# Attention with its fill products in four 32-column quarters, its weight gathers spread and its tail on buffers of its own

## The chip, the cores and the metric

The kernel runs on all 8 cores of one Trainium2 chip, four to a die (cores 0 to 3 and 4 to 7). Each core works alone on its share of the tokens; nothing is exchanged. The metric is the device time of the slowest core in microseconds, as the median of several runs.

## The reference

A sandwich of two residual layers on x of 4 x 4096 x 1024, float32:

```python
x = x + _layernorm(attn(_layernorm(x)))     # 16 heads of 64; Wq, Wk, Wv, Wp, each 1024 x 1024
x = x + _layernorm(ffn(_layernorm(x)))      # one of 8 matrices W[idx], 1024 x 1024, and b[idx]
```

In attn a key takes part if it is not later than the query and its position modulo 4 is not 3; the scores are scaled by 1/8. In ffn, idx is the argmax of log_softmax(logits) plus Gumbel noise made from u, so the matrix is known only at run time.

## The kernel before, in words

Two cores share a batch entry. Each takes every second query (2048) and all 3072 keys that are kept. Work is in bfloat16 with float32 sums.

The **lead** (`lead_units`) transposes the first ten 128-token tiles on TensorE ("T" units), and makes keys of groups 0 and 1 ("K"), values ("V"), the queries of stage 0 ("Q"), norms of both ("N") and from these a bound ("C", the `prodm` product) that goes into each exp as its bias `negc`. Then come four **stages**, one for each 512 queries. Stage t has 8 head pairs of 3t + 2 **pairs of steps**, so 16, 40, 64 and 88 pairs, 208 in all. A step is 128 keys (or two parts of the diagonal) by 512 queries for two heads. A pair goes so:

- `qk(m)`, L725 and L727: scores of both steps, two products of 64 rows by 128 columns side by side. The second buffer is free once the exp of two steps before is done (`s_exp`).
- fills: a part of a `unit`. A unit is a full 128 x 128 product over 8 chunks of the contraction: K (384 wide, L666), Q (L675), V (L682), O, the projection (L701), F, the ffn (L710), each into one of two `pj` banks. Stages 0 to 2 are filled with the next stage's Q, K, V, norm and C units, stage 3 with O and F of query tiles 0 to 11.
- `pv(m-1)`, L762: values. Each of four 128 x 32 products has its own quarter of the columns, with `tile_position=(0, j)`.
- `rowsum(m-1)`, L780: sums of the exps, also in four quarters.

ScalarE does the exps (L1208, 128 x 1024) and part of the evictions; VectorE the other evictions and layer norms; GpSimd masks the diagonal steps (L1320) and issues the weight loads with a cast; SP issues token loads, DMA transposes and stores.

The order of every engine is written by a planner, `make_order`. `spread` lays the fills evenly over 0.94 of a stage's pairs (0.98 in stage 3); `clock` estimates when each pair begins, and every other operation gets a due time, by which the engine queues are sorted. `UNIT_N` numbers the units in TensorE's order; the first `LEAD` of them belong to the lead.

The ffn weights `wfb` lie where `wkb` was. GpSimd gathers them by eight indirect DMAs of 128 rows each (L1388), one behind another, once the last key unit ("K", 7, 7) is done.

The **tail** is the four last query tiles, 12 to 15. `tail_o` makes their projection, `tail_z` and `tail_x` the statistics and the first residual, `tail_ln` the third layer norm, a DMA transpose turns it (SP, "turn"), `tail_f` makes the ffn product (L826 and L828), `tail_fs` and `tail_froot` its statistics, `tail_last` (VectorE, L1085) multiplies and adds, `tail_out` (ScalarE, L1256) subtracts the mean, and the result is stored. The tiles share two staging and two transposed buffers (`ln3t[s % 2]`, `ln3T[s % 2]`), so that the third transpose waits for the first tile's product.

Of the kernel before, what the change touches and what calls it, by code (L numbers as in the profile page):

```python
# [94 lines left out]
def lead_units():  # L95
# [7 lines left out]
    out += v0[:2] + t[6:7] + nk[2:3] + v0[2:4] + t[7:8] + nk[3:] + v0[4:] + t[8:9] + v1[:2] + t[9:]  # L103
    out += q + v1[2:3] + nq[:1] + v1[3:4] + nq[1:] + v1[4:5] + [("C", 0)] + v1[5:]
# [71 lines left out]
def make_order():  # L176
# [133 lines left out]
    z_at, x_at, f_at, last_at = [0.0, 1.4, 5.2, 9.0], [2.8, 6.6, 10.4, 12.8], [15.2, 18.6, 22.0, 26.0], [17.4, 21.0, 24.5, 28.3]  # L310
    for j, s in enumerate(TAIL):
# [7 lines left out]
        dve.append((at + last_at[j], "taillast", s))  # L319
        act.append((at + last_at[j] + 0.6, "tailout", s))  # L320
# [5 lines left out]
    pool.append((end["K", 7, 7] + 0.5, "wf", 0))  # L326
# [54 lines left out]
def build_nc():  # L381
# [109 lines left out]
    ln3t = [ln3, over("ln3t", [128, C], BF16, "wvb", 8192)]  # L491
# [19 lines left out]
    def sem(name):  # L511
        return nc.alloc_semaphore(name=name)
# [83 lines left out]
    s_tfin = sem("s_tfin")  # L596
    s_tdone = sem("s_tdone")
# [24 lines left out]
    def tensor_engine():  # L622
# [31 lines left out]

        def unit(part):
# [5 lines left out]
            if u[0] == "K":  # L661
# [3 lines left out]
                for c in range(c0, c1):  # L665
                    mm = PE.matmul(ps[:, 0:384], wkb[:, c, 128 * e:128 * e + 128], fm[g % 2][:, c, :],  # L666
                                   start=(c == 0), stop=(c == 7))
            elif u[0] == "Q":
# [3 lines left out]
                for c in range(c0, c1):  # L672
                    if t == 0 and e == 0 and c % 4 == 0:
                        PE.wait_ge(s_w["wq", c // 4], 16)
                    mm = PE.matmul(ps[:], wqb[:, c, 128 * e:128 * e + 128], fmQ[:, c, :],  # L675
                                   start=(c == 0), stop=(c == 7))
            elif u[0] == "V":
                _, g, sc, eh = u
                for c in range(c0, c1):
                    if (g, sc, eh) == (0, 0, 0) and c % 4 == 0:  # L680
                        PE.wait_ge(s_w["wv", c // 4], 16)
                    mm = PE.matmul(ps[:], fm[g % 2][:, c, 128 * sc:128 * sc + 128],  # L682
                                   wvb[:, c, 512 * eh:512 * eh + 512], start=(c == 0), stop=(c == 7))
# [9 lines left out]
            elif u[0] == "O":  # L693
# [4 lines left out]
                for c in range(c0, c1):  # L698
                    if s == 0 and eh == 0 and c % 4 == 0:
                        PE.wait_ge(s_w["wp", c // 4], 16)  # L700
                    mm = PE.matmul(ps[:], QY[:, t, c, 128 * j:128 * j + 128],  # L701
                                   wpb[:, c, 512 * eh:512 * eh + 512], start=(c == 0), stop=(c == 7))
            else:
# [3 lines left out]
                for c in range(c0, c1):  # L707
                    if s == 0 and eh == 0:
                        PE.wait_ge(s_wf[c], 16)
                    mm = PE.matmul(ps[:], ln3T[s % 2][:, c, :],  # L710
                                   wfb[:, c, 512 * eh:512 * eh + 512], start=(c == 0), stop=(c == 7))
# [110 lines left out]
        def tail_f(s):  # L822
            PE.wait_ge(s_turn[s % 2], 16 * (s // 2 + 1))
# [723 lines left out]
```

## Time and profile before

| | |
|---|---|
| Three runs, median (lowest, highest) | 762.2 us (761.1 to 763.1) |
| Profiled execution | 765.7 us |
| its span, slowest core (core 1) | 764.6 us |
| its fastest core | 749.4 us |
| TensorE matmuls busy | 669.8 us, 5716 instructions |
| ScalarE busy | 528.8 us |
| VectorE busy | 422.9 us |
| GpSimd busy | 137.5 us |
| instructions in all | 17094 |

The profile is of one execution, on its slowest core unless another is named. In the rows PE is TensorE, PEld its weight loads, DVE VectorE, ACT ScalarE, POOL GpSimd and SP the queue that issues most DMAs. A matmul's start is a time of the profiler, its end is modelled, so costs of matmuls are best read from start to start. "<-" behind a wait names what ended it.

### The profile page before, as it was taken

Reading aid. Unit: us, or ns where it says so; the run is one execution under the profiler, and the core shown is the slowest. Engines: PE = TensorE matmul, PEld = TensorE weight load, DVE = VectorE, ACT = ScalarE, POOL = GpSimd, SP = SyncE. Lnnn points to the kernel's source line nnn. Section 1 sums busy time; section 2 is a strip of 40 time slices with the busy share of each in tenths; the row PEclk is TensorE's granted clock in tenths of the full one; section 3 lists DMA queues with packets and bytes.
Section 4 is the critical chain, followed back from the end, with each engine's and each line's share of the span. In section 5 each row is a group of like instructions: output and inputs, shape, how many; then the busy total and the mean of one; then the engine's idle time right before and its main releaser. Section 6 shows DMA issues by size and latency. Waiting matters only on the chain.

```text
span 764.6 us, 17094 instructions; the slowest of 8 cores (749.4 to 764.6 us)
## 1 busy us (share of the span) xinstructions
PE 669.8 (88%) x5716; PEld 254.0 (33%) x5716; DVE 422.9 (55%) x758; ACT 528.8 (69%) x710; POOL 137.5 (18%) x232
## 2 busy tenths in 40 slices
PE   1788979898999999999999859889999999999855
PEld 1444434343333343333323313222333333332322
DVE  3337667857463634533433213267766766986496
ACT  3342356454898786988787648888888888888246
POOL 1010022223112221112121411110120110750100
PEclk9989999999999999999999979999999999999988
DMA  8889488961653160307000160502222223133314
GB/s 164 177 197 182 99 152 188 181 154 34 150 110 86 28 143 16 72 16 111 27 6 16 40 100 23 174 15 61 79 84 86 71 84 111 30 114 96 119 34 138
DMA packets 78211, 72.00 MB, mean 94 GB/s; under 512 B 58544, under 2 KB 58800, under 8 KB 78128
## 3 DMA queue, kind: packets, MB, share of 16 engines
q1 hardware_dynamic: 72060, 59.50, 30.7%
q0 software_dynamic: 5696, 11.14, 9.4%
q8 instruction: 49, 0.80, 0.4%
q10 hardware_dynamic: 372, 0.27, 0.1%
q14 instruction: 34, 0.28, 0.1%
HBM read 60.68 MB, written 8.52 MB: 90 GB/s over the span
## 4 chain that ended last, share of the span: by engine, by line
PE 59%; ACT 12%; issue 11%; DVE 8%; DMA 6%; another core or an unknown queue 2%; ACTq 1%; SPq 1%; DVEq 0%; POOL 0%; POOLq 0%
PE sps L725 11%; PE yz L762 10%; ACT Pr L1208 9%; PE pj L666 9%; PE pj L682 8%; PE pj L675 5%; PE pj L710 4%; PE yz L780 4%; PE pj L701 4%; DMA zr<-zev 2%; DMA xin<-xkv 1%; DMA fmQ<-tok 1%; PE yz L682 1%; PE yz L675 1%
## 5 line engine op out<-in xcount | busy, mean ns | idle before, releaser
L1208 ACT ACTIVATE Pr<-sps,negc 128x1024 bf16<-128x1024 f32 (+1 forms) x416 | 429.6, 1079 | 115.3 <-PE sps L727 100.0
L1320 POOL TENSOR_TENSOR Pr<-Pr,mk_sb 128x172 bf16<-128x172 bf16 x192 | 100.4, 542 | 497.7 <-ACT Pr L1208 497.6
L725 PE MATMUL sps<-QY,Ksb 64*128 64x512 bf16 (+2 forms) x480 | 137.2, 346 | 23.6 <-ACT Pr L1208 19.1
L727 PE MATMUL sps<-QY,Ksb 64*128 64x512 bf16 (+2 forms) x480 | 138.9, 349 | 0.0
L762 PE MATMUL yz<-Pr,Vsb 128*32 128x512 bf16 (+5 forms) x1920 | 126.5, 349 | 4.7 <-DVE yev L960 2.4
L780 PE MATMUL yz<-Pr,cbf 128*32 128x512 bf16 (+2 forms) x960 | 82.0, 345 | 4.7 <-issue 4.7
L725 PEld LDWEIGHTS sps<-QY,Ksb 64*128 64x128 bf16 x480 | 35.5, 93 | 130.1 <-issue 127.4
L882 DVE TENSOR_TENSOR Vsb<-pj,bvb 128x512 bf16<-128x512 f32 x41 | 28.2, 688 | 68.9 <-PE pj L682 50.4
L762 PEld LDWEIGHTS yz<-Pr,Vsb 128*32 128x32 bf16 x1920 | 31.3, 95 | 86.5 <-issue 84.9
L675 PE MATMUL pj<-fmQ,wqb 128*128 128x512 bf16 x224 | 54.7, 385 | 3.3 <-DMA fmQ<-tok 1.9
L701 PE MATMUL pj<-wpb,QY 128*128 128x512 bf16 x192 | 50.4, 381 | 0.2 <-issue 0.2
L682 PE MATMUL pj<-wvb,fmA 128*128 128x512 bf16 x168 | 41.7, 380 | 5.3 <-DVE Vsb L882 5.3
L666 PE MATMUL pj<-fmB,wkb 128*128 128x384 bf16 x232 | 44.3, 336 | 1.4 <-ACT fmB L1154 1.3
L960 DVE COPY yev<-yz 128x512 f32<-128x512 f32 x32 | 22.1, 690 | 37.6 <-PE yz L780 37.6
L682 PE MATMUL pj<-wvb,fmB 128*128 128x512 bf16 x160 | 40.6, 392 | 0.7 <-DVE Vsb L882 0.7
L666 PE MATMUL pj<-fmA,wkb 128*128 128x384 bf16 x192 | 36.5, 327 | 4.4 <-ACT Ksb L1187 2.1
L1187 ACT ACTIVATE Ksb<-pj,bkc 128x384 bf16<-128x384 f32 x39 | 22.3, 577 | 21.4 <-PE pj L650 11.5
L872 DVE TENSOR_SCALAR tok<-xin,lnst 128x1024 bf16<-128x1024 f32 x33 | 27.9, 846 | 14.4 <-ACT lnst L1150 13.1
L727 PEld LDWEIGHTS sps<-QY,Ksb 64*128 64x128 bf16 x480 | 35.6, 93 | 0.0
L780 PEld LDWEIGHTS yz<-Pr,cbf 128*32 128x32 bf16 x960 | 25.5, 97 | 25.8 <-issue 6.7
L675 PEld LDWEIGHTS pj<-fmQ,wqb 128*128 128x128 bf16 x224 | 19.7, 99 | 32.7 <-issue 14.0
L973 DVE TENSOR_TENSOR QY<-yev,zb 128x512 bf16<-128x512 f32 x32 | 22.8, 712 | 13.6 <-DMA zb<-zscr 13.3
(187 smaller groups left out, 767.4 us busy)
## 6 DMA issues: line engine op xcount, KB each, us to landing
xin<-xkv SPq DMA_DIRECT2D x21, 512.0 KB, 4.8
xr<-xq SPq DMA_DIRECT2D x16, 512.0 KB, 3.4
zb<-zscr SPq DMA_DIRECT2D x62, 128.0 KB, 3.0
xin<-xq SPq DMA_DIRECT2D x12, 512.0 KB, 3.9
out<-xr SPq DMA_DIRECT2D x12, 512.0 KB, 2.9
wkb<-wk POOLq DMA_DIRECT2D x4, 512.0 KB, 17.4
wvb<-wv POOLq DMA_DIRECT2D x2, 1024.0 KB, 14.8
wqb<-wq POOLq DMA_DIRECT2D x2, 1024.0 KB, 14.0
```

Source lines behind the costliest of these rows:

```text
L666: mm = PE.matmul(ps[:, 0:384], wkb[:, c, 128 * e:128 * e + 128], fm[g % 2][:, c, :], start=(c == 0), stop=(c == 7))
L675: mm = PE.matmul(ps[:], wqb[:, c, 128 * e:128 * e + 128], fmQ[:, c, :], start=(c == 0), stop=(c == 7))
L682: mm = PE.matmul(ps[:], fm[g % 2][:, c, 128 * sc:128 * sc + 128], wvb[:, c, 512 * eh:512 * eh + 512], start=(c == 0), stop=(c == 7))
L701: mm = PE.matmul(ps[:], QY[:, t, c, 128 * j:128 * j + 128], wpb[:, c, 512 * eh:512 * eh + 512], start=(c == 0), stop=(c == 7))
L710: mm = PE.matmul(ps[:], ln3T[s % 2][:, c, :], wfb[:, c, 512 * eh:512 * eh + 512], start=(c == 0), stop=(c == 7))
L725: PE.matmul(sps[s % 2][:, 0, off:off + w], Ksb[0:64, g, hp, kc:kc + 128], QY[0:64, t, hp, n0:n0 + w], start=True, stop=True, tile_position ...
L727: mm = PE.matmul(sps[s % 2][:, 1, off:off + w], Ksb[64:128, g, hp, kc:kc + 128], QY[64:128, t, hp, n0:n0 + w], start=True, stop=True, tile ...
L762: PE.matmul(yps[j:j + 32, n0:n0 + w], Vsb[:, c, 64 * h + 32 * half:64 * h + 32 * half + 32], Pr[:, s % 4, hd, off:off + w], start=first, s ...
L780: mm = PE.matmul(zps[j:j + 32, n0:n0 + w], cbf[:, 288:320], Pr[:, (2 * m + a) % 4, hd, off:off + w], start=first and not (a == 1 and k < 8 ...
L882: V.tensor_tensor(out=Vsb[:, 3 * g + sc, 512 * eh:512 * eh + 512], in0=ps[:], in1=bvb[:, 512 * eh:512 * eh + 512], op=ALU.add).then_inc(s_ ...
L1208: A.activation(out=Pr[:, s % 4, :, 0:wide], in_=sps[s % 2][:, :, 0:wide], func=AF.Exp, bias=negc[:, k:k + 1], scale=0.125).then_inc(s_exp, 1)
L1320: op = G.tensor_tensor(out=view, in0=view, in1=mk[:, j:j + 1, :].broadcast_to([128, 2, BAND]), op=ALU.mult)
```

## The change

1. A new function `product` takes the place of the plain matmul in K, Q, V, O and F units behind the lead: four matmuls of 32 columns, each with its tile position.
2. The eight gathers become eight entries of GpSimd's queue, due 5 us apart by the planner, each waiting for the exps that are due before it.
3. In the lead, the values of group 1 go behind the queries, and the first query norm comes in among them.
4. In the tail each tile has staging and transposed buffers of its own, with semaphores of their own, so that `tail_ln` and the transposes wait for no earlier tile. Two small operations per tile leave VectorE for ScalarE. For tiles 12 to 14 the last step is split in another way: ScalarE scales and shifts the product out of PSUM (`tail_scale`), GpSimd adds it to the residual (`tail_sum`); tile 15 keeps the old way. The due times of the last steps follow.

```diff
@@ lead_units
-    out += v0[:2] + t[6:7] + nk[2:3] + v0[2:4] + t[7:8] + nk[3:] + v0[4:] + t[8:9] + v1[:2] + t[9:]
-    out += q + v1[2:3] + nq[:1] + v1[3:4] + nq[1:] + v1[4:5] + [("C", 0)] + v1[5:]
+    out += v0[:2] + t[6:7] + nk[2:3] + v0[2:4] + t[7:8] + nk[3:] + v0[4:5] + t[8:9] + v0[5:] + t[9:]
+    out += q[:7] + nq[:1] + q[7:] + v1[:2] + nq[1:] + v1[2:4] + [("C", 0)] + v1[4:]
@@ make_order
-    ..., f_at, last_at = ..., [15.2, 18.6, 22.0, 26.0], [17.4, 21.0, 24.5, 28.3]
+    ..., f_at, last_at = ..., [15.2, 16.6, 18.0, 22.0], [17.2, 18.6, 20.2, 24.0]
...
+        if s < 15:
+            act.append((at + last_at[j], "tailscale", s))
+            pool.append((at + last_at[j] + 0.6, "tailsum", s))
...
-    pool.append((end["K", 7, 7] + 0.5, "wf", 0))
+    for c in range(8):
+        at = end["K", 7, 7] + 0.5 + 5.0 * c
+        done = sum(begin[m] + 0.4 + 1.1 * a < at for m in range(NP) for a in range(2))
+        pool.append((at, "wf", (c, done)))
@@ tensor_engine
+        def product(u, ps, w, left, right, c):
+            if UNIT_N[u] <= LEAD:
+                return PE.matmul(ps[:, 0:w], left, right, start=(c == 0), stop=(c == 7))
+            for j in range(0, 128, 32):
+                mm = PE.matmul(ps[j:j + 32, 0:w], left[:, j:j + 32], right, start=(c == 0), stop=(c == 7),
+                               tile_position=(0, j))
+            return mm
...
-                    mm = PE.matmul(ps[:, 0:384], wkb[:, c, 128 * e:128 * e + 128], fm[g % 2][:, c, :],
-                                   start=(c == 0), stop=(c == 7))
+                    mm = product(u, ps, 384, wkb[:, c, 128 * e:128 * e + 128], fm[g % 2][:, c, :], c)
...
@@ tail_f
-            PE.wait_ge(s_turn[s % 2], 16 * (s // 2 + 1))
+            PE.wait_ge(s_tturn[s - 12], 16)
@@ tail_x
-            V.tensor_tensor(out=st[:, 48:49], in0=st[:, 12:13], in1=st[:, 15:16], op=ALU.mult).then_inc(s_tx, 1)
...
-            V.tensor_scalar(out=st[:, 49:50], in0=st[:, 28:29], scalar1=-1.0, scalar2=None,
-                            op0=ALU.mult).then_inc(s_txst, 1)
@@ tail_ln
-            if s == 13:
-                A.wait_ge(s_x1, 23)
-            else:
-                A.wait_ge(s_turn[(s - 2) % 2 if s > 12 else 1], 16 * (6 if s == 12 else (s - 2) // 2 + 1))
...
-            A.activation(out=ln3t[s % 2][:], in_=xr[s % 4][:], func=AF.Identity, bias=st[:, 50:51],
+            A.activation(out=st[:, 50:51], in_=st[:, 49:50], func=AF.Identity, scale=-1.0).then_inc(s_txroot, 1)
+            A.wait_ge(s_txroot, 3 * j + 3)
+            A.activation(out=ln3t[j][:], in_=xr[s % 4][:], func=AF.Identity, bias=st[:, 50:51],
@@ scalar_engine
+        def tail_scale(s):
+            j = s - 12
+            A.wait_ge(s_tfroot, 3 * j + 3)
+            for eh in range(2):
+                A.activation(out=tfo[j][:, eh, :], in_=tail_ps[j][:, eh, :], func=AF.Identity,
+                             bias=tst[:, j, 52:53], scale=tst[:, j, 47:48]).then_inc(s_tscale, 1)
@@ pool_engine
+        def tail_sum(s):
+            j, x = s - 12, xr[s % 4]
+            for eh in range(2):
+                half = x[:, 512 * eh:512 * eh + 512]
+                G.wait_ge(s_tscale, 2 * j + eh + 1)
+                G.tensor_tensor(out=half, in0=half, in1=tfo[j][:, eh, :], op=ALU.add).then_inc(s_tsum, 1)
...
+                c, done = key
+                if c == 0:
+                    G.wait_ge(s_sel, 8)
+                    G.wait_ge(s_unit, UNIT_N["K", 7, 7])
+                G.wait_ge(s_exp, done)
+                G.indirect_dma_start(out=wfb[:, c, :], out_offset=None, in_=wf_d,
+                                     in_offset=IndirectOffsetOnAxis(gcol[:, c:c + 1], 0)
+                                     ).then_inc(s_wf[c], 16)
@@ sync_engine
-                if key >= 14:
-                    S.wait_ge(s_ft, 2 * (key - 13))
-                elif key >= 2:
+                if 2 <= key < 12:
                     S.wait_ge(s_unit, UNIT_N["F", key - 2, 1])
```

Q, V, O and F units get the same treatment as K, with a width of 512.

## Rows read from the trace of the kernel before

**Rows 1.** The page: busy time of TensorE's matmuls; the chain's shares by engine.
```profile
PE 669.8 (88%) x5716; PEld 254.0 (33%) x5716; DVE 422.9 (55%) x758; ACT 528.8 (69%) x710; POOL 137.5 (18%) x232
...
PE 59%; ACT 12%; issue 11%; DVE 8%; DMA 6%; another core or an unknown queue 2%; ACTq 1%; SPq 1%; DVEq 0%; POOL 0%; POOLq 0%
```

**Rows 2.** The view of cores: span and granted clock.
```profile
core 1: 764.6 us, clock 0.976
...
core 4: 753.7 us, clock 0.976
```

**Rows 3.** The view by windows, 430 to 460 us, core 1 then core 4.
```profile
430.00:460.00 30.00, 19.78 (x146) 6.14 (x144) 5.03 (x9) 13.86 (x14) 9.83 (x13) 0.83 0.48 80
...
430.00:460.00 30.00, 28.64 (x282) 9.57 (x280) 10.43 (x22) 24.75 (x25) 12.39 (x19) 1.00 0.53 81
```

**Rows 4.** The timeline, GpSimd, 430 to 470 us: the first and last of 8 gathers.
```profile
433.68 1.03 POOL L1388 DMA_INDIRECT wfb<-wf,gcol  x1 [0.85 <-PE pj L666]
...
442.29 0.94 POOL L1388 DMA_INDIRECT wfb<-wf,gcol  x1 [0.27 <-issue]
```

**Rows 5.** The waits, 400 to 500 us: total us, times, longest.
```profile
ACT Pr L1208 <- remote: 11.8, 2, 9.0
```

**Rows 6.** The timeline, TensorE, 701 to 704 us, second scores to next scores.
```profile
701.51 0.37 PE L725 MATMUL sps<-QY,Ksb 64*128 64x512 bf16 x1
...
701.84 1.25 PE L710 MATMUL pj<-wfb,ln3Tb 128*128 128x512 bf16 x5
703.02 0.62 PE L762 MATMUL yz<-Pr,Vsb 128*32 128x512 bf16 x8
703.46 0.39 PE L780 MATMUL yz<-Pr,cbf 128*32 128x512 bf16 x4
703.78 0.39 PE L725 MATMUL sps<-QY,Ksb 64*128 64x512 bf16 x1
```

**Rows 7.** The timeline of the tail: last ffn products, last tile's statistics.
```profile
752.36 1.89 PE L828 MATMUL yz<-wfb,ln3Tb 128*128 128x512 bf16 x8
...
754.30 1.89 PE L828 MATMUL yz<-wfb,ln3Tb 128*128 128x512 bf16 x8
...
757.57 1.28 DVE L1076 BATCH_NORM_STATS2 tst<-yz 128x6 f32<-128x512 f32 x2
```

**Rows 8.** The timeline, TensorE, 425 to 427 us, key chunks and the values behind.
```profile
425.17 1.15 PE L666 MATMUL pj<-fmB,wkb 128*128 128x384 bf16 x6
426.24 0.61 PE L762 MATMUL yz<-Pr,Vsb 128*32 128x512 bf16 x8
```

**Rows 9.** The timeline, TensorE, 712 to 714 us, quarters just after a wait.
```profile
713.04 0.37 PE L762 MATMUL yz<-Pr,Vsb 128*32 128x256 bf16 x8 [0.53 <-POOL Pr L1320]
713.23 0.37 PE L780 MATMUL yz<-Pr,cbf 128*32 128x342 bf16 x8
713.63 0.38 PE L787 MATMUL pj<-brow,bsel 128*128 128x512 bf16 x1
```

**Rows 10.** The page's groups: the weight loads of the values, mean ns of one.
```profile
L762 PEld LDWEIGHTS yz<-Pr,Vsb 128*32 128x32 bf16 x1920 | 31.3, 95 | 86.5 <-issue 84.9
```

**Rows 11.** The waits of TensorE, 310 to 485 us, then 485 to 711 us.
```profile
PE sps L725 <- ACT Pr L1208: 7.7, 20, 1.1
...
PE sps L725 <- ACT Pr L1208: 9.6, 29, 1.0
```

**Rows 12.** The timeline, TensorE, 90 to 98 us: the end of the lead.
```profile
90.68 1.90 PE L682 MATMUL yz<-wvb,fmB 128*128 128x512 bf16 x8
93.09 0.40 PE L688 MATMUL yz<-ksq,cbf 128*32 128x512 bf16 x4 [0.51 <-DVE ksq L904]
93.42 1.90 PE L682 MATMUL pj<-wvb,fmB 128*128 128x512 bf16 x8
97.60 0.17 PE L692 MATMUL pj<-prodm,cbf 128*128 128x8 bf16 x1 [2.27 <-DVE prodm L922]
```

**Rows 13.** The groups by form, GpSimd: a float32 addition of 1024 elements.
```profile
L1339 POOL TENSOR_TENSOR brest<-bfb,brow 128x1024 f32<-128x1024 f32 x1 | 2.1, 2127 | 0.1
```

## What the change will do

> **What bounds the kernel now.** I read the page first, then the cores, then one stretch at a time. The page: TensorE's matmuls cover 88% of the span, and the chain that ended last runs through TensorE for 59% of it, with ScalarE second at 12% [rows 1]. So most of the span belongs to the order in which TensorE takes its work, and a nanosecond saved in each step of it is worth looking for.
>
> The cores come next, because the metric is the slowest. Core 1 sets the time with 764.6; the slowest core of the other die, core 4, has 753.7 [rows 2]. All eight run one program on equal amounts of work, so most of these 10.9 us are lost on one die only. They go between 430 and 460 us: core 1's TensorE is busy 19.78 us of 30 at clock 0.83, core 4's 28.64 at 1.00, with the same DMA share of about 0.5 [rows 3]. In this stretch GpSimd issues the eight gathers of the ffn weights one behind another, one every 1.2 us, from 433.68 to 442.29 [rows 4]; the first mask behind them waits for ScalarE, so GpSimd itself isn't late. ScalarE stood for 11.8 us in two waits that the profile puts down to nothing on the core [rows 5]. I read this as traffic: eight transfers queued at once, and whatever the engines fetch meanwhile stands behind them.
>
> Within a steady pair of steps near 701 us the start times give TensorE's cost of each piece [rows 6]: second scores at 701.51, fills at 701.84, values at 703.02, sums at 703.46, next scores at 703.78. Five fill chunks take 1.18 us to the values' start. A chunk is 0.216 by the tail (eight and one in 1.94 us, 752.36 to 754.30) [rows 7], so 5 x 0.216 = 1.08 and 0.10 is left over. The same comes from the key units: six 384-wide chunks take 1.07 us to the values [rows 8]; at 0.16 each (384/512 of 0.216) that is 0.97, and 0.10 is left. The scores stand 0.33 ahead of the fills and the sums 0.32 ahead of the next scores, where a group of the values takes 0.22. So each change between kinds of array use costs about 0.1 us, and a pair has three: scores (64 rows) to fills (128 x 128), fills to values (128 x 32), sums to scores.
>
> **The change, part by part.** *Fills as quarters.* Each of the 156 units behind the lead has 8 chunks, 1248 in all; a chunk becomes four matmuls of 32 columns, so 3744 matmuls and as many weight loads are added. The fill-to-values change disappears, since both are then 128 x 32. The planner spreads fills over 0.94, 0.94, 0.94 and 0.98 of 16, 40, 64 and 88 pairs: 15 + 38 + 60 + 87 = 200. At 0.095 that is 19.0 us. The 18 norm units behind the lead are quarters already and stand among the fills, with a change on either side; those at the edge of a pair share theirs, so I count some 22 further, 2.1 us. The three bound products stay full width and now have a change in front as well, +0.3 us. Gross on TensorE: 20.8 us.
>
> What does a quartered chunk cost? The trace of before has no such fill, but values and sums have its form. Eight value matmuls (two groups) take 0.44 us, 703.02 to 703.46 [rows 6]: 0.22 a group, beside 0.216 for a full chunk. I take 0 extra; the upper bound is the remainder, 0.01 a chunk, about 13 us over 1248. Below nothing I see no reason. Can TensorE be given eight instructions in 0.216, or in 0.16 for keys? After a wait of 0.53 us, when nothing was queued ahead, 16 matmuls and their loads pass between 713.04 and 713.63 [rows 9]: 32 instructions in 0.59 us, 18 ns each, against 27 and 20 needed. It is enough, for keys only just. A weight load has a mean of 95 ns [rows 10] and must lie beside matmuls: in the value groups four of them fit into 0.22 us, so they do.
>
> *How much of 20.8 us arrives.* TensorE isn't alone in the loop. Two exps of a pair take about 2.12 us, the next but one first score product follows from them, and where the second one of a pair waits for the exp, a fill shorter by 0.1 us is paid back by half at most, as the loop then spans two pairs with one fill in it. Such waits are recorded 20 times from 310 to 485 us and 29 times from 485 to 711 us, 7.7 and 9.6 us [rows 11], and pairs that are just short of them now will begin to wait. So: stage 0 (16 pairs, fed by transposes and by VectorE) half of 2.0, 1.0 us; stage 1 nearly all of its 4.4, less the bound product, 3.8; stage 2 two thirds of 5.9, 3.9; stage 3 two thirds of 8.3, 5.5; the other bound products -0.2. Sum 14.0 us. Bounds: 7 (a third) to 21.
>
> *Gathers spread.* Each of the eight now waits for a count of exps, 5 us behind the one before. Queued behind each on GpSimd are masks, at most one of which is held by an issue of 1.2 us per gather, and values wait a step and a half later; I take 1 us in all for that and for what stays of the traffic. The last gather starts about 35 us behind the first, near 470 us, and the first ffn product is far behind. If the stall goes, core 1 falls to the slowest of the undisturbed die: 764.6 - 753.7 = 10.9, less 1.0, is 9.9 us. Bounds: 3 (it is only thinned) to 11.
>
> *Values behind queries in the lead.* Now the second norm product waits 0.51 us at 93.09 and the bound product 2.27 us at 97.60 [rows 12], since only two value units lie between the last query unit and it. After the change two stand ahead of the second norm product and two more ahead of the bound product, 3.45 us each (two units of 8 x 0.216). The gap at the bound product spans 95.15 to 97.60, the one at the norm product 92.41 to 93.09, so 2.45 + 0.68 = 3.1 us go. The transposes for the next queries are issued once the last query unit is done, and that moves forward by as much (two value units, 3.45, less the one norm product now inside the queries, 0.33), so stage 0 is not left waiting for them: 3.1 us. Bounds 0 to 3.4. The token for the ninth transpose is ready long before, but ScalarE's copy in front of the queries stays bare.
>
> *The tail.* It is VectorE's now: the last tile's products end at 756.2 (754.30 and 1.89), yet its statistics begin only at 757.57 [rows 7]. Three of the four final multiplications leave VectorE for ScalarE and GpSimd; eight small operations go too; with own buffers no transpose waits for products. TensorE's chain of four ffn tiles, 3.9 us each, then sets the end. The last tile's first-half statistics could start by 755.7, as their second half needs 756.3 and one takes about 0.65. 757.57 - 755.7 = 1.8 us. The GpSimd additions, 512 wide, I put at 1.1 us each (half of 2.13 for 1024) [rows 13]; two of tile 14 behind ScalarE end near 758, before the end of tile 15. ScalarE's two additional small operations ahead of each transpose are covered but for some 0.3. Bounds 0.5 to 3.
>
> **Sum.** 764.6 - 14.0 - 9.9 - 3.1 - 1.8 = 735.8 of span; outside it this execution had 1.1 us (765.7), so 736.9. The median shown, 762.2, is 3.5 below this execution; the stall is what differs among cores, so I expect runs with less of it to have less to gain, and leave the forecast at 737.
>
> **Rivals.** (1) The stall stays or moves. TensorE's stream of instructions grows by 7488 on 17094, so more is fetched, and a fetch behind a gather still stands. For: 11.8 us of waits without a source on the core [rows 5]. Against: die 1 has the same gathers and no loss [rows 3]. Price: 5 to 9 us of the 9.9, so 742 to 746. (2) ScalarE's loop takes all in stages 2 and 3: 9.4 us less, 746. For: the waits [rows 11]; against: they are in fewer than half of the pairs. (3) The quarters cost 0.01 more each, 13 us: 750. (4) **Slower**: the four weight loads of a chunk aren't hidden in an unbroken row of fills. Gains of 28.8 us over 1248 chunks are used up at 23 ns each; one bare load of 95 ns a chunk would cost 119 us, and the time would be 856. For: the trace shows at most 24 quartered matmuls in a row between waits. Against: 0.22 a group where values stand [rows 6] and the burst [rows 9]. (5) That the quarters don't remove the change, as the tiles' positions differ by 32 columns within it: values and sums alternate over four positions at 0.22 without any, so I give it nothing apart from (2).
>
> A rule speaks for (4). The Trainium skill's page TensorE: Matmul & The Clock Gate, section The mechanism (Part 3), says that a weight load overlaps running matmuls only where it goes to other row groups; all quarters here span all rows. By that, and by its figure of columns over 1.2 GHz, four loads of 32 columns would add an estimated 107 ns a chunk, some 133 us. The Trainium skill's page TensorEngine Tiling (Array Packing), section Restrictions, adds that column tiling goes without the fast weight load. This case's values contradict the first: 0.22 us a group in the same form [rows 6].
>
> **Chances.** Forecast with its own bounds (729 to 742): 0.60. Rival 1: 0.15. Rival 2: 0.09. Rival 3: 0.08. Rival 4: 0.04, of it nearly all slower. More gained than I allow, under 729: 0.04. Range 729 to 751: it takes in rivals 1 to 3. A measurement of this kernel can tell about 0.3%, 2.3 us, from no change. Faster 0.95, same 0.01, slower 0.04.
>
> **What would show it.** In the profile after: fill matmuls of form 128*32, starts of groups 0.216 apart (0.16 for keys), last fill to values 0.22 instead of 0.31; more waits of the scores on exps in the last two stages; 430 to 470 us with TensorE at clock 1.00 on every core and the dies within a few us; bound product in the lead without its 2.27 us wait; tail with TensorE running to its last ffn product and VectorE's last statistics right behind. Wrong if groups stand at 0.24 or more, if the dies stay 10 us apart, or if ScalarE's idle time does not shrink from 485 to 711 us.

## The result, and the profile after

The changed kernel takes 743.5 us (three runs, 743.47 to 744.73) against 762.2 us (761.14 to 763.13): a ratio of 0.976, 95% interval 0.974 to 0.979. The gain is 18.7 us where 25 were forecast; the time lies 6.5 us above the 737.0 forecast and inside the range of 729 to 751. In some executions of any of these kernels one die shows a lower granted clock and the time is longer (807.6 and 825.3 us for e1_quarters, 809.1 for e3_lead); no comparison below uses them.

The page of the profiled execution after, with its busy times, the instruction fetches, the chain's shares by engine, and the group of the first score product:

```profile
span 741.9 us, 24587 instructions; the slowest of 8 cores (733.8 to 741.9 us)
PE 653.2 (88%) x9460; PEld 284.6 (38%) x9460; DVE 418.6 (56%) x744; ACT 530.2 (71%) x718; POOL 145.0 (20%) x238
...
q8 instruction: 79, 1.29, 0.7%
...
PE 54%; ACT 15%; issue 15%; DMA 8%; DVE 5%; SPq 1%; POOL 1%; ACTq 1%; DVEq 0%; POOLq 0%
...
L744 PE MATMUL sps<-QY,Ksb 64*128 64x512 bf16 (+2 forms) x480 | 138.4, 346 | 25.0 <-ACT Pr L1223 22.9
```

Against [rows 1], matmuls are busy 16.6 us less, with 3744 more of them (the two pages are of different cores, 1 and 6). TensorE's share of the chain falls from 59 to 54% and ScalarE's rises from 12 to 15%. The last row matters most below: 22.9 us of idle before the first score product are ended by an exp. Line numbers have moved: L673 is now the one line of all quartered fills, L744 and L746 are the scores, L781 values, L799 sums, L1223 exps, L1354 masks, L1427 gathers.

The view of cores, after, beside [rows 2]:

```profile
core 1: 733.8 us, clock 0.984
...
core 4: 741.3 us, clock 0.979
...
core 6: 741.9 us, clock 0.975
...
die 0 (median of its cores): 736.2 us, clock 0.983
die 1 (median of its cores): 740.5 us, clock 0.977
```

Core 1, the slowest before, has won 30.8 us and is now the fastest. Core 6, the fastest before at 749.4 us, has won 7.5 and sets the time. To see where, I split each core's span at the starts of its exps in the timeline of ScalarE: the 1st exp, and those of pairs 17, 57 and 121, which begin stages 1 to 3 (exps 33, 113 and 241), and the last (416th). Each column is one execution:

| us | before, core 1 | after, core 1 | before, core 6 | after, core 6 | median of 8, before to after |
|---|---|---|---|---|---|
| first exp | 100.0 | 94.3 | 99.6 | 97.7 | 99.5 to 96.0 |
| stage 0 | 90.0 | 90.5 | 91.0 | 94.4 | 91.3 to 92.6 |
| stage 1 | 120.0 | 117.2 | 118.8 | 116.1 | 120.0 to 117.2 |
| stage 2 | 174.2 | 157.9 | 159.3 | 157.8 | 164.7 to 157.9 |
| stage 3 | 226.6 | 222.2 | 226.2 | 222.4 | 226.3 to 222.1 |
| tail, from the start of the last exp | 53.8 | 51.7 | 54.4 | 53.4 | 54.2 to 52.0 |

Stages 1 to 3 are now nearly the same on all cores (stage 2 takes 157.8 to 158.6 us, where die 0 had 168.8 to 174.2). What separates the cores most is what comes before stage 1: its first exp starts between 184.1 and 192.4 us. The tail adds up to 2 us (51.7 to 53.9).

**A pair of the last stage.** The timeline of TensorE, core 6, five chunks of fill as in [rows 6]:

```profile
679.80 1.26 PE L673 MATMUL pj<-wfb,ln3Tb 128*32 128x512 bf16 x20
680.89 0.61 PE L781 MATMUL yz<-Pr,Vsb 128*32 128x512 bf16 x8
681.32 0.39 PE L799 MATMUL yz<-Pr,cbf 128*32 128x512 bf16 x4
681.64 0.39 PE L744 MATMUL sps<-QY,Ksb 64*128 64x512 bf16 x1
681.65 0.39 PE L746 MATMUL sps<-QY,Ksb 64*128 64x512 bf16 x1
682.07 0.37 PE L744 MATMUL sps<-QY,Ksb 64*128 64x512 bf16 x1
```

Twenty quarters take 1.09 us to the values (679.80 to 680.89), where five full chunks took 1.18. Over all pairs of core 0 the starts of groups of four stand 0.216 us apart in the median (0.163 for products 384 wide), and from the last group to the values it is 0.216 where it was 0.309. But the second pair of scores starts 0.43 us behind the first, where 0.226 is the shortest: it stood for the exp that ends at 681.93 in ScalarE's timeline.

**The gathers.** The timeline of GpSimd, core 6, beside [rows 4]; then 430 to 460 us by windows, core 1 and core 4, beside [rows 3]; then ScalarE's waits on core 1, 400 to 500 us, beside [rows 5]:

```profile
429.15 1.04 POOL L1427 DMA_INDIRECT wfb<-wf,gcol  x1 [1.46 <-ACT Pr L1223]
...
443.93 0.94 POOL L1427 DMA_INDIRECT wfb<-wf,gcol  x1 [3.93 <-ACT Pr L1223]
444.89 2.75 POOL L1354 TENSOR_TENSOR Pr<-Pr,mk_sb 128x172 bf16<-128x172 bf16 x6
...
463.01 0.94 POOL L1427 DMA_INDIRECT wfb<-wf,gcol  x1 [3.06 <-ACT Pr L1223]
```
```profile
430.00:460.00 30.00, 25.27 (x361) 9.02 (x357) 9.27 (x20) 24.76 (x28) 11.58 (x18) 1.00 0.58 125
...
430.00:460.00 30.00, 27.42 (x411) 10.15 (x399) 11.12 (x24) 25.23 (x27) 9.48 (x13) 1.00 0.44 67
```
```profile
ACT Pr L1223 <- PE sps L746: 14.4, 23, 1.3
```

The clock is 1.00 on both dies, ScalarE runs 24.76 us of 30 instead of 13.86, and the two waits that the profile calls "remote" (11.8 us) are gone.

**The lead.** The timeline of TensorE, core 1 and then core 6, beside [rows 12]:

```profile
90.27 0.17 PE L712 MATMUL pj<-prodm,cbf 128*128 128x8 bf16 x1
90.30 1.89 PE L671 MATMUL pj<-wvb,fmB 128*128 128x512 bf16 x8
...
97.09 4.07 PE L673 MATMUL pj<-fmQ,wqb 128*32 128x512 bf16 x72 [2.68 <-DMA fmQ<-tok]
```
```profile
55.54 5.30 PE L671 MATMUL yz<-wvb,fmA 128*128 128x512 bf16 x16 [2.73 <-ACT Ksb L1202]
...
93.25 0.17 PE L712 MATMUL pj<-prodm,cbf 128*128 128x8 bf16 x1
```

The bound product waits no more on either core. Core 6 is 3.0 us behind core 1 there, from one place, before which it was 1.0 us ahead: at 55.54 it had stood 2.73 us for an eviction, and then took 5.30 us for sixteen products which take 3.63 on core 1; its granted clock was 0.50 from 57 to 60 us.

**The tail.** The timeline of TensorE and VectorE on core 1, then TensorE on core 5, beside [rows 7]; and GpSimd's first addition on core 1:

```profile
710.83 3.04 PE L847 MATMUL pj<-wfb,ln3Tt 128*128 128x512 bf16 x8
...
725.57 1.89 PE L847 MATMUL yz<-wfb,ln3Tt 128*128 128x512 bf16 x8
...
727.57 0.70 DVE L1091 BATCH_NORM_STATS2 tst<-yz 128x6 f32<-128x512 f32 x1 [1.24 <-PE yz L847]
```
```profile
711.60 3.62 PE L847 MATMUL pj<-wfb,ln3Tt 128*128 128x512 bf16 x8
...
727.50 1.89 PE L847 MATMUL yz<-wfb,ln3Tt 128*128 128x512 bf16 x8
```
```profile
721.28 2.49 POOL L1346 TENSOR_TENSOR xr<-xr,yev 128x512 f32<-128x512 f32 x2 [37.14 <-ACT yev L1272]
```

On core 1 TensorE runs from tile to tile without a gap, and VectorE's last statistics now wait for it. From the first tile's first eight products (710.83) to the last tile's last eight (725.57) it is 14.7 us; on core 5 it is 15.9, since its granted clock is 0.50 until 716 and the first tile runs longer. Behind the last product 6.3 to 6.8 us are left on all cores, where it was 7.2 to 8.8 before: most of the tail's gain lies there.

### The profile page after: what moved, and what is told of

It reads as the page before. It is cut to its first block, busy times and chain, and to the rows that moved or that the text cites. A ratio compares the mean times of both kernels' runs of the same rounds, so it can differ in the third digit from the quotient of the medians.

```text
span 741.3 us, 24579 instructions; the slowest of 8 cores (733.8 to 741.9 us)
## 1 busy us (share of the span) xinstructions
PE 649.0 (88%) x9452; PEld 283.8 (38%) x9460; DVE 418.1 (56%) x744; ACT 530.2 (72%) x718; POOL 144.0 (19%) x238
## 4 chain that ended last, share of the span: by engine, by line
PE 50%; ACT 15%; issue 15%; DMA 11%; DVE 6%; SPq 1%; ACTq 1%; POOL 1%; DVEq 0%; POOLq 0%
PE pj L673 23%; ACT Pr L1223 12%; PE sps L744 10%; PE yz L781 7%; PE yz L799 4%; DMA wkb<-wk 3%; DMA wvb<-wv 2%; PE yz L671 2%; DMA fmQ<-tok 1%; PE pj L671 1%; PE sps L847 1%; DVE Vsb L901 1%; DMA zr<-zev 1%; DMA xq<-xkv 1%; DMA xq<-xq 1%
## 5 line engine op out<-in xcount | busy, mean ns | idle before, releaser
L1223 ACT ACTIVATE Pr<-sps,negc 128x1024 bf16<-128x1024 f32 (+1 forms) x416 | 428.8, 1078 | 92.7 <-PE sps L746 90.1
L1354 POOL TENSOR_TENSOR Pr<-Pr,mk_sb 128x172 bf16<-128x172 bf16 x192 | 98.9, 536 | 464.8 <-ACT Pr L1223 464.7
L744 PE MATMUL sps<-QY,Ksb 64*128 64x512 bf16 (+2 forms) x480 | 138.7, 346 | 25.2 <-ACT Pr L1223 23.2
L746 PE MATMUL sps<-QY,Ksb 64*128 64x512 bf16 (+2 forms) x480 | 140.4, 350 | 0.0
L781 PE MATMUL yz<-Pr,Vsb 128*32 128x512 bf16 (+5 forms) x1920 | 125.0, 345 | 5.8 <-POOL Pr L1354 3.2
L744 PEld LDWEIGHTS sps<-QY,Ksb 64*128 64x128 bf16 x480 | 35.8, 93 | 133.5 <-issue 131.2
L799 PE MATMUL yz<-Pr,cbf 128*32 128x512 bf16 (+2 forms) x960 | 82.0, 345 | 0.0
L781 PEld LDWEIGHTS yz<-Pr,Vsb 128*32 128x32 bf16 x1920 | 49.4, 97 | 49.3 <-issue 12.5
L673 PE MATMUL pj<-wpb,QY 128*32 128x512 bf16 x768 | 50.7, 381 | 0.1
L673 PE MATMUL pj<-fmQ,wqb 128*32 128x512 bf16 x768 | 48.0, 388 | 2.2 <-DMA fmQ<-tok 2.2
L673 PE MATMUL pj<-wvb,fmA 128*32 128x512 bf16 x576 | 38.2, 394 | 5.0 <-DVE Vsb L901 5.0
L673 PE MATMUL pj<-fmA,wkb 128*32 128x384 bf16 x768 | 36.7, 327 | 3.8 <-ACT Ksb L1202 2.5
L673 PE MATMUL pj<-wvb,fmB 128*32 128x512 bf16 x576 | 35.5, 381 | 0.8 <-DVE Vsb L901 0.8
L673 PE MATMUL pj<-fmB,wkb 128*32 128x384 bf16 x768 | 36.0, 327 | 0.1
L746 PEld LDWEIGHTS sps<-QY,Ksb 64*128 64x128 bf16 x480 | 36.1, 93 | 0.0
L992 DVE TENSOR_TENSOR QY<-yev,zb 128x512 bf16<-128x512 f32 x32 | 23.9, 748 | 16.6 <-DMA zb<-zscr 16.4
L799 PEld LDWEIGHTS yz<-Pr,cbf 128*32 128x32 bf16 x960 | 25.8, 97 | 19.5 <-issue 0.9
L673 PEld LDWEIGHTS pj<-fmQ,wqb 128*32 128x32 bf16 x768 | 18.5, 98 | 26.6 <-issue 13.0
```

Source lines behind the costliest of these rows:

```text
L673: mm = PE.matmul(ps[j:j + 32, 0:w], left[:, j:j + 32], right, start=(c == 0), stop=(c == 7), tile_position=(0, j))
L744: PE.matmul(sps[s % 2][:, 0, off:off + w], Ksb[0:64, g, hp, kc:kc + 128], QY[0:64, t, hp, n0:n0 + w], start=True, stop=True, tile_position ...
L746: mm = PE.matmul(sps[s % 2][:, 1, off:off + w], Ksb[64:128, g, hp, kc:kc + 128], QY[64:128, t, hp, n0:n0 + w], start=True, stop=True, tile ...
L781: PE.matmul(yps[j:j + 32, n0:n0 + w], Vsb[:, c, 64 * h + 32 * half:64 * h + 32 * half + 32], Pr[:, s % 4, hd, off:off + w], start=first, s ...
L799: mm = PE.matmul(zps[j:j + 32, n0:n0 + w], cbf[:, 288:320], Pr[:, (2 * m + a) % 4, hd, off:off + w], start=first and not (a == 1 and k < 8 ...
L992: V.tensor_tensor(out=QY[:, t, hp, :], in0=yev[:, k % 2, :], in1=zb[:, k % 2, :], op=ALU.mult).then_inc(s_ynorm, 1)
```

## The experiments

Numbers of stages below are medians over the eight cores. "Before" was timed again on the chip of each group of runs.

**1. The parts alone.** Four kernels, each the kernel before with one part of the change. Only the lines that matter are shown.

```diff
e1_quarters: K, Q, V, O and F units by
+            for j in range(0, 128, 32):
+                mm = PE.matmul(ps[j:j + 32, 0:w], left[:, j:j + 32], right, start=(c == 0), stop=(c == 7),
+                               tile_position=(0, j))
```

> The kernel before with the quartered fills alone. Theory A (the quarters' 20.8 us on TensorE arrive for about a third, since the exps' loop takes the rest): 7 to 9 us less than before, about 754, with the stall of the gathers still there and the dies still some 10 us apart. Rival B (they arrive for two thirds, as predicted, and another part of the change gave less): 13 to 15 us less, about 748. Rival C (a stream of 44% more instructions suffers more from the gathers' traffic): under 5 us less, with the stall longer than before on die 0 or on both dies.

Two runs gave 756.3 and 761.0 us, where before gave 763.2 to 769.0 on that chip. That is too few for a ratio, so I read the profiled run by stage: stage 0 92.7 (no gain), stage 1 117.0 (120.0 in the profile of before, 118.8 in that of the next kernel), stage 3 222.2 (4 less); stage 2 on die 1 156.7 (2.7 less) and on die 0 166.3, still with the stall. This is nearest to theory A. The stall isn't longer (7.6 to 7.8 us a core, 6.6 to 11.8 before), against rival C. No group of quarters costs more than the full chunk did. That ends rival 3 (0.01 us more each) and rival 4 (bare weight loads, 856 us).

```diff
e2_gathers:
-    pool.append((end["K", 7, 7] + 0.5, "wf", 0))
+    for c in range(8):
+        at = end["K", 7, 7] + 0.5 + 5.0 * c
+        done = sum(begin[m] + 0.4 + 1.1 * a < at for m in range(NP) for a in range(2))
+        pool.append((at, "wf", (c, done)))
```

> The kernel before with the gathers spread alone. Theory A (the stall is the traffic of eight queued gathers, on die 0 only): core spans of die 0 fall to those of die 1, die 1 stays; time 8 to 10 us less, about 753. Rival B (the stall is something of die 0 that only happens to fall there): the dies stay some 10 us apart, time within 2 us of before.

758.1 us, ratio 0.989 (0.985 to 0.993): 8.4 us (5.4 to 11.2). Stage 2 takes 160.5 to 161.2 us on all cores. It was 168.8 to 174.2 on die 0 and 159.3 to 160.7 on die 1, so the stall is gone, and the spreading itself costs about 1.3 us (medians of die 1: 159.4 to 160.6).

```diff
e3_lead:
-    out += q + v1[2:3] + nq[:1] + v1[3:4] + nq[1:] + v1[4:5] + [("C", 0)] + v1[5:]
+    out += q[:7] + nq[:1] + q[7:] + v1[:2] + nq[1:] + v1[2:4] + [("C", 0)] + v1[4:]
```

> The kernel before with values behind queries alone. Theory A: the first exp comes about 3 us earlier, 97 instead of 100 us, and the time falls by 2 to 3 us. Rival B (stage 0 hangs on its transposes and tokens, and gives the 3 us back before stage 1): the first exp earlier, stage 1 at the same time as before, time within 1 us.

762.6 us, ratio 0.996 (0.994 to 0.999): 2.8 us (0.9 to 4.7), near the 3.1 forecast. The timeline of TensorE, core 1:

```profile
90.50 0.17 PE L692 MATMUL pj<-prodm,cbf 128*128 128x8 bf16 x1
...
97.78 3.57 PE L675 MATMUL pj<-fmQ,wqb 128*128 128x512 bf16 x8 [3.02 <-DMA fmQ<-tok]
```

The bound product is 7 us earlier than in [rows 12] and doesn't wait, but the first fill of stage 0 then stands 3.02 us for the transposes of the next queries, where it stood 1.9 before. In the median over the cores the first exp comes 3.1 us earlier and stage 1 begins 1.7 us earlier (190.7 to 189.0): stage 0 gives part of the gain back, as rival B said, but not all.

```diff
e4_tail: buffers of their own, scaling on ScalarE, addition on GpSimd, nothing else
+    tfo = [yev, zev, zb]
+    ln3t = [over(f"ln3t{i}", [128, C], BF16, "QY", 8192 + 2048 * i) for i in range(4)]
+    ln3Tt = [over(f"ln3Tt{i}", [128, 8, 128], BF16, "QY", 16384 + 2048 * i) for i in range(4)]
```

> The kernel before with the new tail alone. Theory A (TensorE's chain of four ffn tiles becomes the bound): from the last exp to the end 52 us instead of 54, time 1.8 us less. Rival B (it depends on when TensorE's clock comes back after 9 us of idle time): 0 to 2.5 us by core, since with own buffers nothing else is left in front of it, and the slowest core may have none of it.

763.5 us, ratio 0.9965 (0.994 to 0.999): 2.7 us (1.0 to 4.4). Its tail is 52.2 us, from 51.7 to 53.6, against 54.2 before.

**2. The quarters, with everything else in place.** The changed kernel with full-width fills.

```diff
e5_after_full:
-            for j in range(0, 128, 32):
-                mm = PE.matmul(ps[j:j + 32, 0:w], left[:, j:j + 32], right, ..., tile_position=(0, j))
-            return mm
+            return PE.matmul(ps[:, 0:w], left, right, start=(c == 0), stop=(c == 7))
```

> The changed kernel with fills at full width again, everything else of the change kept. Theory A (the quarters arrive for under half of TensorE's 20.8 us): 8 to 10 us slower than the changed kernel, about 752, of it 4 in stage 3, 2 to 3 in stage 2, 2 in stage 1, none in stage 0. Rival B (14 us arrive): about 757.

752.7 us (751.9 to 754.2), ratio 0.985 (0.983 to 0.986). By medians the quarters are worth 9.2 us (752.7 less 743.5); by the two ratios, each against its own runs of before, 6.5. The last three stages, which are free of the lead's spread, give 1.5, 2.9 and 4.1, in sum 8.6 us before rounding. Over all profiled executions with whole exps, those with quarters against those with full fills, stage 1 differs by 1.6 us in the median and 2.3 in the mean, and stage 3 by 4.1 and 4.2. The prediction had 14.0. The row of the page for the first score product:

```profile
L739 PE MATMUL sps<-QY,Ksb 64*128 64x512 bf16 (+2 forms) x480 | 136.9, 346 | 18.9 <-ACT Pr L1218 16.5
```

It stands 16.5 us for exps with full fills and 22.9 with quarters: 6.4 us of the saving have turned into this wait. These are the slowest cores of two executions; averaged over the eight cores, such waits are 2.0, 5.2 and 9.6 us in stages 1 to 3 with full fills and 2.6, 7.6 and 12.8 with quarters. To check the books of one stage I summed, on core 0, the shortest spacing of each kind of neighbouring groups over stage 3: 203.3 us with full fills and 194.3 with quarters, 8.9 less before rounding. (These two sums depend somewhat on how kinds are told apart.) Between the two pairs of scores the time beyond the shortest spacing grows from 18.6 us (55 times) to 23.0 (58 times). 8.9 less 4.4 is 4.5, and the stage is 4.1 shorter.

**3. Is it the exps?** If that wait takes the saving back, shorter exps should let it through. In both kernels each exp covers half its columns (the other half of the tile holds ones).

```diff
e6_short, e7_full_short:
+            wide = wide // 2
             A.activation(out=Pr[:, s % 4, :, 0:wide], in_=sps[s % 2][:, :, 0:wide], func=AF.Exp,
```

> The changed kernel with each exp over the first half of its columns only (the other half of the weights stays at 1, so the output isn't the reference's). Theory A (the scores' wait for the exps takes what the quarters save): with exps of half the length nothing waits for them; stage 3 takes about 196 us instead of 222, which is what its TensorE groups add up to, and stage 2 about 138. Rival B (VectorE or the evictions hold the loop): stage 3 stays over 210 us.

> The same short exps, with fills at full width. Theory A: stage 3 takes 8 to 9.5 us longer than with quarters and short exps (87 changes of 0.093 and the values' groups), against 4.1 with whole exps; stage 2 some 6 us longer. Rival B (the loop isn't the reason; the saving of a pair is itself only 0.05): stage 3 about 4 us longer as with whole exps.

The times are 712.0 us with quarters and 723.2 with full fills, one run each: 11.2 us. Neither expectation came true as it stood. With quarters stages 2 and 3 take 146.2 and 203.7 us, not the 138 and 196 of theory A, and stage 3 does not stay over 210 as rival B has it; full fills make them 4.3 and 5.1 us longer, where theory A had 6 and 8 to 9.5 and rival B 4 in stage 3. By stage the quarters give 3.3, 4.3 and 5.1, in sum 12.8 us before rounding, where they gave 8.6 with whole exps. The 5.1 is loose: stage 3 differs by 4.6 us among the cores of the one execution and by 6.4 among those of the other. The page's rows, quarters first:

```profile
L744 PE MATMUL sps<-QY,Ksb 64*128 64x512 bf16 (+2 forms) x480 | 126.2, 350 | 2.5 <-ACT Pr L1225 2.1
```
```profile
L739 PE MATMUL sps<-QY,Ksb 64*128 64x512 bf16 (+2 forms) x480 | 124.5, 348 | 1.6 <-ACT Pr L1220 1.1
```

The wait is nearly gone in both, and 4.2 us more arrive. So ScalarE's loop does take part of the saving; it explains about 4 us of the 11 that are missing against the sum of shortest spacings (an estimate of 20.0 us for stages 1 to 3 from core 0: 4.5, 6.6 and 8.9). With half exps 12.8 of those arrive. The last 7 are not in one wait. In stage 3 of core 0 idle beyond the shortest spacings is 7.1 us with full fills and 11.5 with quarters, spread over scores to scores (1.5 to 3.1), fill to fill (1.1 to 2.8) and smaller ones. I have no cause for these that a run has shown.

**4. How far must the gathers stand apart?** The changed kernel with the gathers in one row, in two rows of four, and 2.5 us apart.

```diff
e11_together:
-        at = end["K", 7, 7] + 0.5 + 5.0 * c
...
+    pool.append((end["K", 7, 7] + 0.5, "wf", 0))
e10_fours:
+        at = end["K", 7, 7] + 0.5 + 20.0 * (c // 4)
e9_spacing:
+        at = end["K", 7, 7] + 0.5 + 2.5 * c
```

> The changed kernel with the eight gathers in one row again, the rest of the change kept. Theory A (the stall is that row's, whatever else changed): stage 2 at 165 to 170 us on die 0 and 156.5 on die 1, the slowest core some 8 us above the changed kernel, about 750. Rival B (die 0 lost time for another reason): as the changed kernel.

> The changed kernel with the gathers in two rows of four, 20 us apart. If the stall starts only with a long queue: stage 2 within 1 us of 157.9 on both dies. If it goes with the bytes that are queued: two stalls of together 4 to 9 us on die 0.

> The changed kernel with the gathers due 2.5 us apart instead of 5. At 5 us stage 2 takes 157.9 us on every core, 1.4 more than 156.5, which die 1 had with quarters and the gathers in one row. Theory A (the stall needs more than two or three gathers queued, and the 1.4 us are the masks behind gathers and longer traffic): stage 2 at 156.5 to 157.5 on both dies, time 0 to 1 us less than the changed kernel. Rival B (the stall comes from any gather's traffic that overlaps the next): the stall is back on one die, stage 2 over 160 there.

| gathers | time, us | stage 2, die 0 | stage 2, die 1 |
|---|---|---|---|
| eight in a row | 753.1 (one run) | 165.1 to 170.2 | 156.4 to 157.6 |
| two rows of four | 746.3 (one run) | 164.3 to 166.6 | 156.4 to 159.2 |
| 2.5 us apart | 746.3 (742.4 to 749.3) | 157.2 to 158.6 | 157.2 to 159.3 |
| 5 us apart (the change, other chip) | 743.5 | 157.8 to 158.6 | 157.8 to 157.9 |

ScalarE's waits on core 1 from 400 to 500 us, eight in a row and then two rows of four; and eight in a row by windows, core 1:

```profile
ACT Pr L1220 <- remote: 11.3, 3, 7.0
```
```profile
ACT Pr L1223 <- remote: 7.9, 2, 4.1
```
```profile
430.00:460.00 30.00, 22.04 (x242) 7.10 (x242) 6.11 (x11) 14.42 (x14) 9.28 (x14) 0.77 0.50 80
```

Four in a row stop ScalarE on all four cores of die 0 twice, 7.3 to 7.9 us in sum. Eight in a row stop it on all 20 cores of die 0 in the five kernels that have them (before, e1_quarters, e3_lead, e4_tail, e11_together), 4.7 to 11.8 us in sum. At 2.5 or 5 us apart no core of eight kernels has such a wait. So what is queued together matters, not that the same transfers run. On the 20 cores of die 1 with eight in a row ScalarE has no such wait; one of them (core 4 of e3_lead) lost about 6 us at the same place, where TensorE stood 4.5 us for VectorE and VectorE 8.8 us for the small DMA `zr<-zev`. Why mostly one die suffers, though both issue the same gathers, no run here tells.

"Remote" is only the profile's word for a wait whose end it can't place. In the kernel an exp waits for `s_qk` and `s_pv`, and TensorE alone raises both. So in those waits ScalarE waited for TensorE's counts, and the prediction's reading, nothing on the core, is wrong. The timeline of TensorE in the kernel before, core 1, and its DMA queues from 441.8 to 465.7 us:

```profile
441.11 0.37 PE L725 MATMUL sps<-QY,Ksb 64*128 64x512 bf16 x1 [2.27 <-issue]
...
446.63 0.38 PE L780 MATMUL yz<-Pr,cbf 128*32 128x512 bf16 x1 [2.07 <-issue]
449.65 0.63 PE L780 MATMUL yz<-Pr,cbf 128*32 128x512 bf16 x3 [2.65 <-issue]
```
```profile
q0 software_dynamic: 747, 1.34, 35.6%
q1 hardware_dynamic: 365, 0.27, 4.2%
```

TensorE stands three times, 7.0 us in all, for nothing that the profile shows ("issue"), and ScalarE's wait ends at 449.97. On core 3 no such gap is drawn: TensorE's matmuls end by 443.6 and the exp starts at 448.99. That the stopped engine waits for its instructions, as the prediction has it, was not tested, and this trace gives it no support: on core 1 no packet of an instruction queue moves in the 24 us that hold the end of the stall. The gathers' packets alone don't stop an engine either: they take 103% of the 16 engines' time on core 1 from 442 to 449.9 us and on core 6, which doesn't stop, from 434 to 442. What stops TensorE stays open.

The 2.5 us version is not shown to be faster: its ratio is 0.974 (0.970 to 0.979) against 0.976 (0.974 to 0.979), and its stage 2 (medians 158.0 and 157.7 on the two dies) misses the 156.5 to 157.5 of theory A. In its profiled execution the slowest core had a late first exp (100.1) and a stage 0 of 96.6.

**5. The cold first tile of the tail.** Dummy products while TensorE waits for the first transposed tile.

```diff
e8_warm:
+            for event, n, count in ((s_tx, 1, 10), (s_txst, 1, 8), (s_tln, 1, 11)):
+                PE.wait_ge(event, n)
+                for _ in range(count):
+                    PE.matmul(tail_ps[0][:, 0, :], bsel[:], brow[1][:, 0:512], start=True, stop=True)
```

> The changed kernel with 29 products more while TensorE waits for the first transpose of the tail (they write a bank that is overwritten; 10 behind the residual, 8 behind its statistics, 11 behind the third layer norm). Theory A (the tail's length now hangs on when TensorE's clock comes back): granted clock 1.00 in the first ffn tile, which takes 3.9 us instead of 5.2 to 6.4, and the time falls by 1.3 to 2.5 us against the changed kernel, 741 to 742. Rival B (the chain of transposes, one each 3 to 5 us, holds the later tiles): the first tile shorter, the end at the same time.

743.0 us (740.9 to 745.0), ratio 0.972 (0.969 to 0.975), against 0.976 (0.974 to 0.979): the intervals overlap, so no gain is shown. TensorE on core 4:

```profile
714.59 0.38 PE L853 MATMUL pj<-brow,bsel 128*128 128x512 bf16 x1 [0.85 <-DMA ln3Tt<-ln3t]
714.80 1.89 PE L855 MATMUL pj<-wfb,ln3Tt 128*128 128x512 bf16 x8
...
718.97 0.38 PE L853 MATMUL sps<-brow,bsel 128*128 128x512 bf16 x1 [0.33 <-DMA ln3Tt<-ln3t]
...
723.41 0.38 PE L853 MATMUL sps<-brow,bsel 128*128 128x512 bf16 x1 [0.40 <-DMA ln3Tt<-ln3t]
...
729.45 1.89 PE L855 MATMUL yz<-wfb,ln3Tt 128*128 128x512 bf16 x8
```

The first eight products now take 1.89 us instead of 3.04 or 3.62 (on all eight cores), and the next two tiles wait for their transposes instead, which come every 4.4 us: 714.80 to 729.45 is 14.7 us, what core 1 had without the dummies. The tail is 51.2 to 52.8 us, median 52.1, against 52.0. So the tails of 53.4 to 53.9 are gone in this execution, and nothing else is gained.

```diff
e12_both: e8_warm and e9_spacing together
```

> The changed kernel with gathers 2.5 us apart and the 29 warming products in the tail. If both bring what their theories say: 741 to 742 us. The warming products alone gave 743.0 (740.9 to 745.0), no measurable difference; the cores' stage 0 varies by some 6 us between cores and decides which is slowest.

744.6 us (741.3 to 745.6), ratio 0.974 (0.971 to 0.977). Stage 2 is 157.1 to 158.4 on both dies and the tail 51.1 to 53.2. The 741 to 742 us did not come, and nothing adds up to a version that measurably beats the change.

## Why the prediction came out as it did

**The forecast of 737.0 was 6.5 us too low, and most of it is one term, the quarters.** The terms of 28.8 us were taken from the profiled 765.7; against the median before, 762.2, the forecast gain was 25.2 and the measured one is 18.7. Term by term, each as its own run or its stages show it:

| term | forecast | measured | from |
|---|---|---|---|
| quarters | 14.0 | 8.6 (6.5 or 9.2 by the times) | e5_after_full against the change |
| gathers | 9.9 | 8.4 (5.4 to 11.2) | e2_gathers |
| lead | 3.1 | 2.8 (0.9 to 4.7) | e3_lead |
| tail | 1.8 | 2.7 (1.0 to 4.4) | e4_tail |
| sum | 28.8 | 22.5 | |

The parts, measured one at a time, add up to 3.8 us more than the whole. Their intervals allow that, and a gain on the slowest cores counts only down to the next. The differences of the stages' medians, in the table at the top, add up to about 18.

*The gross saving of the quarters was right,* but for a slip: the shares of the four stages add up to 20.6 where 19.0 and 2.1 make 21.1. A group stands at 0.216, my value of 0 extra and not the upper bound; the change between kinds of array use is gone (0.309 to 0.216), and a small gain unasked for (value group to value group 0.227 before, 0.216 now).

*The step that failed is "how much of 20.8 us arrives".* I granted nearly all of stage 1, two thirds of stages 2 and 3 and half of stage 0: 1.0, 3.8, 3.9 and 5.5. It was 0, 1.5, 2.9 and 4.1. For the last two stages the mechanism was the one named, the second scores' wait for an exp [rows 11], but it took more than a third: in stage 3, 4.4 of 8.9 us. The reading behind "fewer than half of the pairs" was wrong. The view behind [rows 11] counts a wait only from the modelled end of the matmul before, 0.37 to 0.39 us behind its start, and shows none under 0.15 us: 29 waits, 9.6 us. By start times, on the same core in stage 3, scores come later behind the scores before them than the shortest spacing in 55 of 103 places, by 18.7 us in all, and what second scores wait for is an exp. So in more than half of these places the exp already ended last. I had argued that a shorter fill is paid back by half at most and only in pairs that already wait. Here it was paid back by half over the whole stage. Rival 2 put that in its strong form (all of stages 2 and 3, 746 us); the truth lies between it and the forecast. Stage 1 was called nearly free, but 1.5 of 4.5 us arrived there, with half exps 3.3; waits for exps grow by only 0.6 us in it, so that mechanism doesn't explain its loss. Stage 0 gave nothing; I read it as set by its feeding (after the change TensorE waits there 5.2 us for evictions of values, 2.2 for transposed queries and 2.1 for `yev`, averaged over the cores), which no run took away.

Of the prediction's three signs of being wrong none came: groups stand at 0.216, the dies are 4.3 us apart, and ScalarE's idle time in stage 3 shrinks, from 31.2 to 27.5 us on core 0.

*The gathers: right in effect and, within the interval, in size; the mechanism is open.* The stall went, on every core of die 0, and rival 1 (the stall stays or moves) is refuted although 79 instruction packets are fetched instead of 49 (cores 6 and 1). What is left is the cost of spreading: masks are queued behind gathers on GpSimd (443.93, then six masks from 444.89), and in stage 2 the values of e2_gathers once stand 1.0 us for a mask (cores 5 and 6), which doesn't happen there in the kernel before. I put 1 us; die 1, which had no stall to lose, shows 1.3, and with quarters 1.2 (156.7 in e11_together, 157.9 in the change).

*The lead: right up to the first exp, but stage 0 gives part of it back.* Over the eight cores the first exp comes 3.5 us earlier in the median, against 3.1 forecast. The prediction said that stage 0 is not left waiting for the transposes; it does wait (3.02 us instead of 1.9 in e3_lead, core 1) and is 1.3 us longer, and the end of stage 0 varies by 8.3 us among the cores after, where it varied by 5.6 before. The forecast followed core 1, and for core 1 it was close: 29 us against 30.8. The time is that of core 6, which won 7.5: 1.9 at the first exp, -3.4 in stage 0, 2.7, 1.5, 3.8, and 1.0 in the tail. I should have made the sum for a core of the undisturbed die as well, and asked what its first 190 us vary by.

*The tail: as forecast within the interval, with two sizes off.* It is 1.9 us shorter in e4_tail and 2.2 in the change, by medians. TensorE's chain sets the end as said. GpSimd's addition of 512 takes 1.24 us and not 1.1, off the path for tiles 12 to 14. I took 3.9 us for every tile; the first one takes 5.2 to 6.4, since the granted clock is 0.50 at its start, but this costs only cores 5 to 7, as the later tiles' transposes are no earlier.

*Rivals 3 and 4* are out: twenty quarters with their loads take 1.09 us against 1.18 for five full chunks and a change, 72 in a row take 4.07 us, and the extra of a chunk is 0. The rule that spoke for rival 4 (the Trainium skill, TensorE: Matmul & The Clock Gate, The mechanism (Part 3)), that a weight load lies beside matmuls only where it goes to other row groups, disagrees with this: all quarters span the same 128 rows. The estimate that the prediction worked out by it was 107 ns more a chunk; measured is 0.

## What to carry to other kernels

Where two forms of matmul alternate, count the changes between them in the start times (0.09 us each here), and then the waits that sit just behind them, for in the last stage these took back half of what the changes gave. Count those waits in start times as well: a view that counts from a modelled end showed 29 where there were 55. Gathers that one engine issues one behind another, 1.2 us apart, stopped others here; 2.5 us between them were enough. Make the sum for the fastest core as well as for the slowest, since a gain on the slowest counts only down to the next.

## What the runs showed of the hardware

- With four gathers of 128 rows queued in a row ScalarE waits for TensorE's counts on die 0 by up to 4.1 us at a time, with eight by up to 9.3, while the gathers' packets fill the 16 DMA engines (103% of their time on core 1); 2.5 us apart it doesn't. On die 1 the engines are as full, and one core in 20 lost time there.
- Groups of four matmuls of 32 columns of the array, with their four weight loads, start as often as single ones of 128 columns: every 0.216 us for a width of 512, every 0.163 for 384, in rows of 72 matmuls as well.
- From a matmul of 128 columns to one of 32 columns it is 0.309 us instead of 0.216; between two of 32 columns for different products it is 0.216.
- After 8.9 us without work the first eight products of the tail took 3.0 to 3.6 us at a granted clock of 0.50 instead of 1.89; kept busy until then they took 1.89, on all 16 cores of e8_warm and e12_both. The median tail didn't move (52.1 and 52.0 us), since transposes came every 4.4 us.
